# Returning expert rows into one array by token, with adding DMAs, instead of into two arrays

## What is computed

```python
x = x + conv_block(layernorm_over_channels(x))
t = tokens(x)                                  # [128, 81, 256], n = 10368 tokens of 256 channels
xf = layernorm(t)
probs = softmax(xf @ Wr.T + br)                # 8 experts
top2_prob, top2_idx = top_k(probs, 2)
h = gelu(xf @ W1[e] + b1[e])                   # 256 -> 512
o = h @ W2[e] + b2[e]                          # 512 -> 256
t = t + sum over the token's two experts of  prob * o
```

## Time and profile before

| | us |
|---|---|
| median of 3 runs | 1727.75 |
| lowest and highest | 1718.6, 1734.06 |
| profiled execution, its own time | 1730.86 |
| profiled execution, span of the core | 1729.1 |
| mean granted TensorE clock in it | 0.841 of full |

### The profile page before, as it was taken

One profiled execution on the slowest core, in us unless ns is written; L12 is line 12 of the kernel. 1 busy time (PEld: TensorE's weight loads), 2 busy tenths in 40 slices (PEclk: granted clock), 3 DMA queues, 4 the chain that ended last, 5 costly groups with the idle time before them and its releaser, 6 DMA issues.

```text
span 1729.1 us, 36819 instructions
## 1 busy us (share of the span) xinstructions
PE 1290.2 (75%) x9688; PEld 1082.9 (63%) x9689; DVE 1123.5 (65%) x2536; ACT 772.5 (45%) x1820; POOL 570.6 (33%) x561
## 2 busy tenths in 40 slices
PE   0393989878999999997664710699999999999200
PEld 0383888875666666666664610588888888888200
DVE  6894333435778788887467652477777777777593
ACT  0491444434445444442557770355455554545100
POOL 0260111113443343432227777233333333333100
PEclk9996878788999999997555555799999999999655
DMA  8534445358787787782224344222222232222575
GB/s 303 125 92 180 162 162 191 143 190 188 185 188 168 179 191 173 178 203 58 89 68 151 132 149 169 78 83 92 92 89 95 79 95 89 91 93 72 204 295 246
DMA packets 258510, 251.04 MB, mean 145 GB/s; under 512 B 150010, under 2 KB 234447, under 8 KB 255205
## 3 DMA queue, kind: packets, MB, share of 16 engines
q1 hardware_dynamic: 238159, 197.25, 38.8%
q0 software_dynamic: 20320, 53.45, 9.0%
HBM read 152.34 MB, written 105.75 MB: 149 GB/s over the span
## 4 chain that ended last, share of the span: by engine, by line
PE 54%; DVE 21%; issue 7%; ACT 6%; DMA 5%; POOL 3%; DVEq 1%; SPq 1%; ACTq 0%; POOLq 0%
PE ps L678 14%; PE ps L663 13%; PE ps L486 5%; DVE big L1187 4%; PE ps L452 4%; POOL rows_d L1447 3%; ACT pool_ L1227 2%; PE ps L647 2%; PE ps L530 2%; PE ps L503 2%; PE ps L468 2%; DVE aux L975 2%; PE ps L513 2%; ACT aux L1320 2%; DVE pool_ L733 1%
## 5 line engine op out<-in xcount | busy, mean ns | idle before, releaser
L1456 POOL DMA_INDIRECT y_d<-pool_,to_s x176 | 173.8, 987 | 359.4 <-ACT pool_ L1373 330.1
L678 PE MATMUL ps<-pool_,aux 128*128 x2112 | 248.9, 274 | 5.1 <-DVE aux L1149 3.2
L663 PE MATMUL ps<-aux,pool_ 128*128 128x256 f16 x2112 | 247.2, 274 | 0.8 <-ACT aux L1366 0.6
L678 PEld LDWEIGHTS ps<-pool_,aux 128*128 128x128 f16 x2112 | 199.4, 98 | 48.6 <-issue 23.6
L663 PEld LDWEIGHTS ps<-aux,pool_ 128*128 x2112 | 206.2, 98 | 26.5 <-issue 1.8
L1447 POOL DMA_INDIRECT rows_d<-aux,idx_s x162 | 160.9, 993 | 118.9 <-ACT aux L1322 72.0
L1366 ACT ACTIVATE aux<-ps,b_s 128x256 f32<-128x256 f32 x352 | 138.4, 475 | 96.5 <-DVE aux L1149 48.3
L1358 ACT ACTIVATE aux<-ps 128x512 f16<-128x512 f32 x88 | 52.6, 597 | 202.2 <-PE ps L647 202.2
L1441 POOL DMA_DIRECT2D pool_<-v_d x64 | 50.1, 783 | 226.8 <-PE ps L563 222.9
L503 PE MATMUL ps<-pool_,se_w_s 81*81 81x512 f32 x256 | 118.8, 607 | 7.2 <-DMA pool_<-k_d 7.2
L1157 DVE SCALAR_TENSOR_TENSOR pool_<-ps,pool_ 128x512 f32<-128x512 f32 x88 | 60.9, 692 | 95.2 <-PE ps L678 95.2
(11 more groups left out here) (199 smaller groups left out, 2863.7 us busy)
## 6 DMA issues: line engine op xcount, KB each, us to landing
pool_<-rows_d SPq DMA_DIRECT2D x88, 260.0 KB
pool_<-y_d SPq DMA_DIRECT2D x18, 1152.0 KB, 9.4
big<-in_x SPq DMA_DIRECT2D x2, 5184.0 KB, 20.9
xn_d<-big SPq DMA_DIRECT2D x16, 648.0 KB, 3.0
v_d<-aux SPq DMA_DIRECT2D x64, 162.0 KB, 1.9
ks_d<-aux SPq DMA_DIRECT2D x64, 162.0 KB, 1.9
pool_<-xn_d SPq DMA_DIRECT2D x32, 324.0 KB
pool_<-k_d SPq DMA_DIRECT2D x32, 324.0 KB
```

Of the source, the lines that this page charges most:

```text
L663: last = nc.tensor.matmul(o, w_s[:, a, bass.ds(e * (4 * PIECE) + (k * HID + j * 128), 128)], xh_s[:, par, b, k * SLOTS:(k + 1) * SLOTS], s ...
L678: last = nc.tensor.matmul(ps[:, 6 + par, s * C:(s + 1) * C], hh_s[:, par, a, j, s * 128:(s + 1) * 128], w_s[:, b, bass.ds(e * (4 * PIECE) ...
L1456: nc.gpsimd.indirect_dma_start(out=y_d[:, :], out_offset=bass.IndirectOffsetOnAxis(ap=to_s[:, par, k:k + 1], axis=0), in_=yo_s[:, par, k, ...
```

## The change

`y_d` becomes one array by token with a spare block of 256 rows at its end. SyncE writes zeros over it, at the beginning of the routing stage, behind the wait for `x1_c` and ahead of the loads of `b2` and of the weights; for this `zero_s` is cleared on VectorE at the end of the convolution block and not at the end of routing. The returns are indirect DMAs with `compute_op` add, both choices of a token to the same row. An adding DMA reads its destination and writes it back, so two tiles that hold the same token may not overlap: GpSimd issues a tile's returns only after those of the tile before have landed. Within a tile, of one expert, a token stands at most once. Padding rows now go to the spare block, with no bounds check; the index no longer depends on the choice. The tail loads one array and makes one addition per chunk.

```diff
-        y_d = dram("y_d", [2 * TOKENS, C])
+        y_d = dram("y_d", [TOKENS + SLOTS, C])
@@ SyncE
             sp.wait_ge(S["x1_c"], GROUPS + CREDIT)
+            sp.wait_ge(S["zero_c"], 1)
+            nought = zero_s[:, 0:1, 0:C]
+            sp.dma_start(y_d[0:TOKENS, :].rearrange("(b q) c -> b q c", q=HW),
+                         nought.to_broadcast([128, HW, C])).then_inc(S["nought"], 16)
+            sp.dma_start(y_d[TOKENS:, :].rearrange("(s b) c -> b s c", b=128),
+                         nought.to_broadcast([128, SLOTS // 128, C])).then_inc(S["nought"], 16)
             sp.dma_start(b2_s, bass.AP(ffn_b2.tensor, 0, [[0, 128], [1, EXPERTS * C]])).then_inc(S["b2_in"], 16)
...
-                for k in range(2):
-                    rows = y_d[k * TOKENS:(k + 1) * TOKENS, :].rearrange("(b q) c -> b q c", q=HW)
-                    sp.dma_start(got_s[:, n % 4, k], rows[:, n * CHUNK_P:(n + 1) * CHUNK_P, :]
-                                 ).then_inc(S[f"gat{n % 4}"], 16)
+                rows = y_d[0:TOKENS, :].rearrange("(b q) c -> b q c", q=HW)
+                sp.dma_start(got_s[:, n % 4, 0], rows[:, n * CHUNK_P:(n + 1) * CHUNK_P, :]
+                             ).then_inc(S[f"gat{n % 4}"], 16)
@@ VectorE
             add_band(GROUPS - 1)
+            nc.vector.memset(zero_s[:, :, :], 0.0).then_inc(S["zero_c"], 1)
+            dve.wait_ge(S["zero_c"], 1)
             link(nc.vector.tensor_copy(base_s[:, :], region_s[:, :]))
...
-            link(nc.vector.memset(zero_s[:, :, :], 0.0))
             nc.vector.memset(zero_s[:, :, C:C + 1], -1.0)
...
-                nc.vector.scalar_tensor_tensor(to_s[:, par], here_s[:, 1], -float(TOKENS), first,
-                                               ALU.mult, ALU.add).then_inc(S["idx2_c"], 1)
+                nc.vector.tensor_copy(to_s[:, par], first).then_inc(S["idx2_c"], 1)
...
-                dve.wait_ge(S[f"gat{n % 4}"], 32 * (n // 4 + 1))
-                for k in range(2):
-                    ins = nc.vector.tensor_tensor(sums, sums, got_s[:, n % 4, k].rearrange("b q c -> b c q"), ALU.add)
-                    if k == 0:
-                        ins.then_inc(S["mix_d"], 1)
-                        dve.wait_ge(S["mix_d"], n + 1)
-                ins.then_inc(S["fin_d"], 1)
+                dve.wait_ge(S[f"gat{n % 4}"], 16 * (n // 4 + 1))
+                nc.vector.tensor_tensor(sums, sums, got_s[:, n % 4, 0].rearrange("b q c -> b c q"),
+                                        ALU.add).then_inc(S["fin_d"], 1)
@@ GpSimd, return_rows
-                        in_=yo_s[:, par, k, :], in_offset=None, bounds_check=2 * TOKENS - 1, oob_is_err=False).then_inc(S[f"yst{par}"], 16)
+                        in_=yo_s[:, par, k, :], in_offset=None, compute_op=ALU.add).then_inc(S[f"yst{par}"], 16)
-            with pool.Fori(0, TILES // 2) as i:
+            pool.wait_ge(S["nought"], 32)
+            return_rows(0, 0)
+            pool.wait_ge(S["yst0"], 32)
+            return_rows(1, 1)
+            with pool.Fori(1, TILES // 2) as i:
                 for par in range(2):
+                    pool.wait_ge(S[f"yst{1 - par}"], 32 * (i + par))
                     return_rows(i * 2 + par, par)
@@ constants on the host
-    token[:, :, 1] = TOKENS + np.arange(TOKENS).reshape(BS, HW)
-    pad = 2 * TOKENS + np.arange(SLOTS, dtype=np.float32).reshape(-1, 128).T
+    token[:, :, 1] = np.arange(TOKENS).reshape(BS, HW)
+    pad = TOKENS + np.arange(SLOTS, dtype=np.float32).reshape(-1, 128).T
```

More of the change, by code:

```diff
@@ L234, in metaformer_kernel @@
                    l2_p l2m_c e_c band_p x1_c phase_a wst_in0 wst_in1 wst_in2 whi_c wlo_c b2_in rm_p rw_c
-                   blk_p part_c turned_c lgr_c var2_c ln_c rstd_c nmr_c probs_c ex2_c tot_c tri_p xft_c idx_c
+                   blk_p part_c turned_c lgr_c var2_c ln_c rstd_c nmr_c probs_c ex2_c tot_c tri_p xft_c idx_c zero_c nought
                    """ + " ".join(f"scat{k}" for k in range(RING)) + """ yw_c ends_c base_c pad_out tab_r rin0 rin1 tt_p xhi_c xlo_c h_p
-                   gel_c hhi_c hlo_c w2_p yo_c tag_c idx2_c yst0 yst1 gat0 gat1 gat2 gat3 mix_d fin_d
+                   gel_c hhi_c hlo_c w2_p yo_c tag_c idx2_c yst0 yst1 gat0 gat1 gat2 gat3 fin_d
                    out_s meta_c settle_s"""
```

## The result

| | median us | ratio to before, 95% interval |
|---|---|---|
| before | 1725.3 | |
| after | 1820.7 | 1.055 (1.048 to 1.062) |
| forecast | 1695 (1686 to 1760) | 0.981 |

A forecast was written before the change was run, and what follows sets the result against it. GpSimd's scatters bound routing, TensorE the tile loop, VectorE the tail. Span 1729.1 - 39.6 (tail) + 6.2 (zeroing) + 1.1 (last landing) = 1696.8 us, so a median of about 1695 us, range 1686 to 1760.

The forecast's parts named there:

- Tail: After the tile loop: one load and one addition fewer per chunk shorten 81.55 us to 41.9, saving 39.6 us.
- last landing: After the last tile: the adding return's longer landing is not hidden, costing 1.1 us once.
- Zeroing: Routing: stores of 10.88 MB on SyncE's queue ahead of bias and weights delay piece 0, and the tile loop, by 6.2 us.
- Returns: Tile loop: adding returns landing in 3.5 us, under a room of 4.47 us, stay hidden behind TensorE: 0 us.
- its bounds (2.4 to 5.3): Landing of an adding return: 2.4 us if adding costs nothing, 5.3 us with a whole DRAM load before the store.
- The room: Tile loop: landing, counted from the second return's issue, may take 4.47 us before GpSimd is late.
- Rival C: Tile loop: landing over 4.47 us makes the chain of returns the bound, period 1.29 us plus landing; 1766 to 1817; chance 0.24.
- Rival B: Routing: zeroing from one re-read row is slower than the scatters, +19 us (1708), at the slow bound 1736; chance 0.12.
- the bounds for the zeroing: Routing: the zeroing stores take 25.4 us (delay +1.0) by the fast bound, 71.6 us (+47) by the slow bound.
- half rate for an adding transfer: Tile loop: two sources read through one ring make a return's 0.37 us of data 0.74, landing 2.8 us, still inside the room.
- a landing of 4.8 us: Tile loop: an added read at high load, 2.4 + 0.4 + 2.0 us, would make the time some 28 us more.

The follow-up runs named there:

- e2: After with adds kept, but even and odd tiles adding into two arrays, so GpSimd skips the wait for the preceding tile: 1714.5 us, ratio 0.995.
- e1: After with the add taken out of the returns (plain stores), same order, waits, zeroing and tail: 1694.5 us, ratio 0.981.
- e8: After with an array of half the width: returns, zeroing and tail loads carry 128 of 256 columns, same row count: 1761.2 us, ratio 1.021.
- e4: After with GpSimd's loop of returns unrolled, every wait against a constant: 1804.5 us, ratio 1.046.
- e3: After with both zeroing stores moved on SyncE's queue behind the last weight piece: 1813.3 us, ratio 1.050.
- e5: After with the zeroing cut into nine stores behind weight pieces 4 to 12, the spare block behind piece 13: 1803.8 us, ratio 1.047.
- e9: Kernel with waits only at changes of expert and spread zeroing (ratio 0.983), plus three of nine tail additions moved to GpSimd: 1710.8 us, ratio 0.989.

## Why the prediction was wrong, step by step

**Tail, last landing.** Right: -40.2 for -39.6 us, nine additions of 4.03 us, 5.1 us from the loads' issue to the first (1743.62 to 1748.73); +1.6 for +1.1 us, with the last landing at 3.69 us for 3.5.

**Zeroing.** The mechanism was right, the size short: 10 us at the second batch (8.8 at the first return) for 6.2. The two stores of 10.88 MB landed 37.7 us after the first's issue, where the sum had 35.3 with the scatters beside them. The bias, issued only at 847.7 as SyncE was held, and piece 0 took 4.9 us more, where the sum had 3.1. ScalarE waited 10.35 us for that piece:

```profile
861.05 0.63 ACT L1330 ACTIVATE pool_<-pool_ 128x512 f16<-128x512 f32 x1 [10.35 <-DMA pool_<-in_ffn_w]
```

**Returns.** This step failed. The forecast had the returns at 0 us in the loop, hidden behind TensorE; they cost 1.35 us a tile, 118.5 us in all. Three terms of the chain were wrong.

| term | forecast | measured in after |
|---|---|---|
| from the first issue's start to the second's | 1.29 | 1.85 |
| landing from the second issue's start | 3.5 | 4.4 |
| GpSimd from landing to the next issue | not there | 1.0 |
| sum | 4.8 | 7.2 |
| TensorE's period | 5.8 | 5.8 |

(Measured: medians in 1300 to 1600 us; the period over the whole loop is 7.19 us.)

The issue of an adding DMA had been given +0 to +0.3 us, by the spread of plain ones; it was +0.57 (median 0.986 us in before, 1.55 in e2, 1.59 in after), outside what was called a bound. Slow instances of an operation bound nothing for another operation. The landing was inside its bounds (2.4 to 5.3), 3.8 us for a tile's first return, close to the value taken, and 4.4 for the second, which is the one that counts. As landing is counted from the start of the issue, 0.6 us of its growth over the plain 2.4 us is again the dearer issue.

The third term is the error of method, and with 1.0 us the largest. The room was read as 1313.38 - 1308.91 = 4.47 us, issue to issue, and compared with the landing alone. But an engine that is released by a semaphore needs time until its next instruction starts, and the rows show how much: ScalarE's weighted rows end at 1311.61 + 0.89 = 1312.50 and GpSimd's return starts at 1313.38, 0.88 us later. With it the room is 3.6 us, and 3.0 once the issue has grown by 0.57. At the forecast's own 3.5 us of landing the loop would have been just hidden by the first and 0.5 us late by the second; the 1 us to spare that the forecast saw (4.47 less 3.5) was never in the rows.

**Rival C** was the right one, with its place, its signs and its formula but for the missing term, and had 0.24; its price at a landing of 5.3 us and issues 0.3 us longer, 1817 us, meets the measured 1821 by luck, with terms that are wrong singly (5.6 + 1.6 against 4.4 + 1.85 + 1.0). By its formula the measured issues and landing alone, 1.85 + 4.4 = 6.25 us, would be 0.5 us over TensorE's period in 85 tiles, an estimate of 1737 us and inside the range; the missing 1.0 us puts the time beyond 1760. Rival B and the bounds for the zeroing did not matter.

**The engines' time, and the load.** The Trainium skill's half rate for an adding transfer ("Collectives: The Full Stack", "The bandwidth ceiling: the fold count") speaks in the right direction and is too mild here; the Trainium skill says it of ReduceScatter in rings of three and more ranks, and the forecast had carried it over to an indirect DMA. The profile's row of the queue of GpSimd's DMAs (packets, MB, share of 16 engines), e1 and then e2:

```profile
q0 software_dynamic: 20320, 55.28, 9.5%
```
```profile
q0 software_dynamic: 37216, 55.28, 18.1%
```

9.5% of 1695 us is 161 us of all engines, 18.1% of 1715 is 310: 149 us more for 23.1 MB that took 67 us as plain stores, by the queue's mean. By this estimate an adding return takes about 3.2 times the engines' time, not twice. With the Trainium skill's 2 us for an access under high load ("DMA: Bandwidth & Descriptors", "Latency and other measured facts") the forecast had worked out a landing of 4.8 us. In e2, at a DMA share of 0.56, landing was at most 4.0 us, and the second returns that landed after 4.4 us did so at a share of 0.44: the later landings do not go with the higher share.

## What to carry to other kernels

When a change adds a wait, write out the whole ring that it closes, and sum all of it: issues, landing, and the waiting engine's own time from release to its next instruction, which stands in the trace wherever that engine is released by another; then compare with the period. An operation that the trace doesn't hold may cost more in its issue than any instance of its plain form. And ask for which iterations an ordering is needed: restricted to those, and with the zeroing spread, the same change gained 1.7% instead of losing 5.5%.

## What the runs showed of the hardware

- An adding indirect DMA of 128 rows of 1 KB from SBUF to DRAM: 1.55 us of GpSimd and 3.8 us from the issue's start to landing (e2), against 0.96 and 2.4 us for the plain one (e1). With a wait for each tile's returns the second of two landed after 4.4 us (after). With rows of 512 bytes 1.56 us, 3.3 and 3.9 us (e8).
- GpSimd took 1.0 us from the landing of a DMA to the start of the next indirect one behind three waits, 0.15 us of it loop work (after, e4).
- A store behind a long store held SyncE itself: the 256 KB store behind 10.6 MB took 28.5 us (after) and 40.9 us (e3) to issue, half of it behind half the bytes 16.6 us (e8), and all that SyncE would have issued meanwhile came later. Cut into ten and put between loads, the same bytes cost nothing (e5).
- Additions that read two SBUF arrays did not run on VectorE and GpSimd at the same time: one of 4.05 us took 9.93, one of 6.6 us took 21.92 (e9).
- Writes of 1 KB runs from one re-read row of SBUF reached 326 GB/s at a DMA share of 0.96 (818 to 846 us of after).
